# Four graph layers on one core: where VectorE pools gathered neighbours, and where one pair's keys are made

## What is computed

```python
# layer 0: maximum over the first 25 neighbours of each node
scores = where(adj != 0, -arange(N), -inf)
vals, idx = top_k(scores, 25)
agg = max over the 25 of x[idx]          # missing ones are -inf
agg = where(degree <= 25, maximum(agg, 0), agg)
out = relu(concat([x, agg]) @ W + b)
# layers 1 and 2: graph attention (softmax of masked leaky_relu scores, elu)
# layer 3: attention weights from x @ att_W @ x.T, masked by adj == 1, softmax;
for W, b in ((W0, b0), (W1, b1)):        # two attention steps with the same weights
    x = tanh(att @ (x @ W + b))
```

## Time and profile before

| what | value |
|---|---|
| median of 3 runs | 1952.48 us (1941.37 to 1954.05) |
| the profiled execution's own time | 1933.09 us |
| its span, first to last instruction | 1931.0 us |
| mean granted TensorE clock | 0.952 of full speed |
| PE / PEld busy | 1671.2 us (87%) / 1316.0 us (68%) |
| DVE busy | 1429.5 us (74%) |
| ACT busy | 1127.9 us (58%) |
| POOL busy | 1445.9 us (75%) |

### The profile page before, as it was taken

The page is one execution under the profiler, slowest core; times in us unless marked ns, Lnnn a source line. Parts: engine busy times, 40 slices in busy tenths (PEclk is TensorE's granted clock), DMA queues, the critical chain, the costliest instruction groups (busy, mean ns, idle before and its releaser), DMA issues.

```text
span 1931.0 us, 29391 instructions
## 1 busy us (share of the span) xinstructions
PE 1671.2 (87%) x9767; PEld 1316.0 (68%) x9812; DVE 1429.5 (74%) x3427; ACT 1127.9 (58%) x1517; POOL 1445.9 (75%) x2135
## 2 busy tenths in 40 slices
PE   4777798999889898999989899998989898896777
PEld 2655676777759676677758677686757777595747
DVE  5874888768877789768886788768887688746531
ACT  6664755656665765656565665558556665652252
POOL 6888888888888888888788888888878887870000
PEclk9998899989999999998999999998999999997889
DMA  7231424343343333344233333435233522311010
GB/s 195 71 84 37 103 78 100 90 125 78 77 131 73 103 78 98 107 99 111 73 119 86 102 79 76 129 77 127 72 102 87 121 57 63 107 36 33 1 66 12
DMA packets 153282, 167.06 MB, mean 87 GB/s; under 512 B 102685, under 2 KB 119978, under 8 KB 153130
## 3 DMA queue, kind: packets, MB, share of 16 engines
q1 hardware_dynamic: 119594, 96.43, 18.6%
q0 software_dynamic: 33536, 68.75, 13.5%
HBM read 140.45 MB, written 4.19 MB: 75 GB/s over the span
## 4 chain that ended last, share of the span: by engine, by line
PE 43%; DVE 27%; ACT 9%; POOL 8%; issue 7%; DVEq 6%; DMA 1%; ACTq 0%; SPq 0%; POOLq 0%
PE spare L903 11%; PE big L1150 6%; POOL gathered L563 6%; PE big L1011 5%; DVEq L73 4%; PE big L1087 3%; PE big L935 3%; DVE probs_t L1454 3%; PE big L1109 3%; DVE pooled L1327 3%; ACT hot L632 2%; PE side L1127 2%; POOL pause L568 2%; DVE keys L1224 2%; PE big L1002 2%
## 5 line engine op out<-in xcount | busy, mean ns | idle before, releaser
L563 POOL DMA_INDIRECT gathered<-in_x_dram,rows x1048 | 1089.3, 1039 | 240.1 <-issue 158.4
L903 PE MATMUL spare<-hot,x_part 128*128 128x512 f32 x1552 | 393.4, 405 | 36.2 <-DVE hot L1375 27.3
L568 POOL MEMSET pause<- 32x256 bf16 x1048 | 349.9, 334 | 41.9
L903 PEld LDWEIGHTS spare<-hot,x_part 128*128 128x128 f32 x1552 | 291.4, 193 | 108.9 <-issue 21.2
L632 ACT ACTIVATE hot<-running,minus_count 128x2048 fp32r<-128x2048 bf16 (+1 forms) x131 | 251.1, 1916 | 131.8 <-PE spare L903 112.8
L635 ACT ACTIVATE hot<-hot,plus_one 128x2048 fp32r<-128x2048 f32 (+1 forms) x131 | 251.5, 1920 | 4.3
L1011 PEld LDWEIGHTS big<-values,probs_t 128*128 128x128 f32 x1792 | 219.8, 199 | 8.6
L1011 PE MATMUL big<-values,probs_t 128*128 128x129 f32 x1792 | 222.7, 283 | 0.4
L1327 DVE TENSOR_REDUCE pooled<-gathered 128x128 f32<-128x2048 f32 (+2 forms) x56 | 212.0, 3786 | 14.3 <-DMA gathered<-in_x_dram,rows 13.3
L1375 DVE TENSOR_SCALAR hot<-running 128x2048 fp32r<-128x2048 bf16 (+1 forms) x145 | 186.4, 1305 | 33.9 <-PE spare L903 16.4
L1454 DVE SCALAR_TENSOR_TENSOR probs_t<-side,col_gain,adj_t 128x1024 f32<-128x1024 f32 x128 | 154.6, 1276 | 27.3 <-ACT side L691 27.3
(11 more groups left out here) (203 smaller groups left out, 2629.5 us busy)
## 6 DMA issues: line engine op xcount, KB each, us to landing
adj_in<-in_adj_dram SPq DMA_DIRECT2D x128, 512.0 KB, 3.7
gathered<-in_x_dram,rows POOLq DMA_INDIRECT x1048
xs<-in_x_dram SPq DMA_DIRECT2D x8, 512.0 KB, 4.7
out_dram<-xs SPq DMA_DIRECT2D x8, 512.0 KB
adj_t<-adj_bf SPq DMA_TRANSPOSE x64
packed_t<-group_bits SPq DMA_TRANSPOSE x28, 2.8
w_sb<-in_L_gnn_W_dram SPq DMA_DIRECT2D x1, 128.0 KB
w_sb<-in_L_gnn_W_dram SPq DMA_DIRECT2D x2, 64.0 KB
```

Source lines behind the costliest of these rows:

```text
L563: (late_gathered if late else rows_gathered[t % RING]).raised_by(pool.indirect_dma_start(out=gathered[:, t % RING, k * C:(k + 1) * C], out ...
L568: last = nc.gpsimd.memset(pause[quarter:quarter + 32, k // (4 * PAUSED), :], 0.0)
L903: last = nc.tensor.matmul(pick_bank(b, q), x_parts[part][:, m, :], hot[:, place_of(b, q, m), :], start=(m == 0 and part == 0), stop=(m == ...
```

## The change

Three of the poolings move, and one pair's packing and keys.

- Pool 4 moves from "steps" into the attention loop, a new place "tile 5" behind the row maximum of tile 5.
- Pool 6 moves from "last step" to the end of "steps", ahead of `max_pick` 11.
- Pool 7 moves from "end" to "last step", and that place moves: it now stands behind hot 13 and ahead of `max_pick` 13.
- The keys of pair 1 move. They were made for graph b+1 in graph b's "layer 0"; now they are made for graph b+2 in graph b's second attention step, at a new place "turned" behind `max_pick` 13. For graph 1 they are made in the start (`FIRST_WORK` 22).
- PE's packing for them moves from behind tile 7 of the second step to behind tile 1, ahead of pick 13; ACT's `take_fed` 3 moves to directly behind the conversion, ahead of hot 14.
- With "end" empty, the layer norm stands ahead of `max_pick` 15.

```diff
--- before.py
+++ after.py
@@ -101,12 +101,12 @@
               17: [("members b", 1, 0), ("members c", 1, 0)],
               18: [("pool", 0, 4)],
               20: [("pool", 0, 5)],
+              22: [("keys", 1, 1)],
               24: [("pool", 0, 6)],
               26: [("pool", 0, 7)]}
 FEED_PLACE = {0: 0, 1: 1, 2: 2, 3: 7}
 FEED = {0: (1, 2), 1: (1, 3), 2: (2, 0), 3: (2, 1)}
-SIDE = {"layer 0": [("keys", 1, 1)],
-        "gat 1": [("members", 1, 1)],
+SIDE = {"gat 1": [("members", 1, 1)],
         "gat 1 heads": [("keys", 1, 2), ("pool", 1, 0)],
         "gat 2": [("members", 1, 2)],
         "gat 2 heads": [("pool", 1, 1), ("keys", 1, 3)],
@@ -115,9 +115,10 @@
         "tile 1": [("members b", 1, 3)],
         "tile 2": [("members c", 1, 3), ("pool a", 1, 3)],
         "tile 3": [("pool b", 1, 3)],
-        "steps": [("pool", 1, 4), ("keys", 2, 0), ("members", 2, 0), ("pool", 1, 5)],
-        "last step": [("pool", 1, 6)],
-        "end": [("pool", 1, 7)]}
+        "tile 5": [("pool", 1, 4)],
+        "steps": [("keys", 2, 0), ("members", 2, 0), ("pool", 1, 5), ("pool", 1, 6)],
+        "last step": [("pool", 1, 7)],
+        "turned": [("keys", 2, 1)]}
 
 
 def gathered_slots(b, t):
@@ -764,6 +765,7 @@
                     first_ready.raised_by(nc.scalar.copy(xt[:, halves[h]], side[:, halves[h]]))
                 take_xw(b, 1, high_t)
                 feed(b, slot, 3, in_loop)
+                take_fed(b, 3, in_loop)
                 if exists(b, 1, B, in_loop):
                     make_hot(b + 1, 14)
                 act.wait_ge(first_ready.sem, first_ready.at(b, 2))
@@ -774,7 +776,6 @@
                     last = nc.scalar.activation(head[:, t, :], low_t[:, t, :], ACT.Tanh, scale=recip[:, t:t + 1])
                     if t % HALF == HALF - 1:
                         att_tanh.raised_by(last)
-                take_fed(b, 3, in_loop)
                 if exists(b, 2, B, in_loop):
                     for j in range(T):
                         take_count(b + 2, 0, j)
@@ -1151,11 +1152,12 @@
                                                 start=(m == 0), stop=(m == T - 1))
                     if t % HALF == HALF - 1:
                         att_heads.raised_by(last)
+                    if t == 1 and exists(b, 2, B, in_loop):
+                        feed(b, slot, 3, in_loop)
                     if t in (1, 5) and exists(b, 1, B, in_loop):
                         spare_maxed(b + 1, 12 + t // HALF)
                         pick(b + 1, 13 + t // HALF)
                 if exists(b, 1, B, in_loop):
-                    feed(b, slot, 3, in_loop)
                     pick(b + 1, 15)
                     if exists(b, 2, B, in_loop):
                         spare_maxed(b + 1, 14)
@@ -1502,7 +1504,6 @@
 
             def graph(b, slot, in_loop):
                 flat = xs[slot][:, :, :].rearrange("p t c -> p (t c)")
-                side_work(b, slot, "layer 0", in_loop)
                 for h in range(2):
                     dve.wait_ge(pooled_turned.sem, pooled_turned.at(b, h + 1))
                     pooled_t_ready.raised_by(nc.vector.tensor_tensor(pooled_t[:, halves[h]], high[:, halves[h]],
@@ -1543,11 +1544,13 @@
                 if picks:
                     max_pick(b + 1, 11)
                     make_hot(b + 1, 12)
-                side_work(b, slot, "last step", in_loop)
                 if picks:
                     max_pick(b + 1, 12)
                     make_hot(b + 1, 13)
+                side_work(b, slot, "last step", in_loop)
+                if picks:
                     max_pick(b + 1, 13)
+                side_work(b, slot, "turned", in_loop)
                 for h in range(2):
                     dve.wait_ge(att_tanh.sem, att_tanh.at(b, 2 + h + 1))
                     link(nc.vector.tensor_tensor(
@@ -1558,10 +1561,9 @@
                         if picks:
                             make_hot(b + 1, 15)
                             max_pick(b + 1, 14)
-                side_work(b, slot, "end", in_loop)
+                layer_norm(slot)
                 if picks:
                     max_pick(b + 1, 15)
-                layer_norm(slot)
 
             def pack_first():
```

## The result

The changed kernel takes 1980.35 us (median of four runs, 1975.45 to 1985.73) where the kernel before takes 1951.01: a ratio of 1.0163, interval 1.0128 to 1.0199, or +29.3 us. It is slower, as forecast; the forecast was 1993.5, +41.

A forecast was written before the change was run, and what follows sets the result against it. Bound mainly by the string pick 15, counts, layer norm half, `take_xt`, conversion, hot 0. Graph 0's 13.8 plus 27.5 for graphs 1 to 5 gave +41: 1952.5 + 41 = 1993.5 us, chance 0.55, range 1950 to 2014 (forecast's own 1980 to 2005).

The forecast's parts named there:

- mechanism: Second attention step: DVE stands at pool 7 for tile 7's rows, delaying `max_pick` 13, picks 14 and 15: +41 us in all.
- Its size: DVE's stand at pool 7 for gathered rows: some 12 us in each of graphs 1 to 5, 20 in graph 0.
- The landing itself: Graph 2, POOL's gathers: tile 7's last ends at 841.74, its rows land 1.6 us later, at 843.3.
- The graph's term of 5.5: Each of graphs 1 to 5 loses 4.6 to 6.2 us, taken as 5.5: 27.5 together.
- The lucky profile: Whole span: the profiled execution's 19.4 us below the median was taken as common to both kernels, giving 1993.5 instead of 1974.
- Graph 0: Second step: POOL's rate alone sets it; pick 14 comes 14.6 us later, less 0.8: +13.8.
- Graph 6: No packing or keys behind; wait alike, but pool 7 no longer ahead of its layer norm: 0, bounds -4 and +6.
- The packing: Ahead of pick 13: PE stands 0.9 us for the transpose, bounds 0 and 5.0, hidden by pool 7's wait: cost 0.
- Layer norm and L1508: Graph's end and layer 0: ACT's 0.36 us wait goes; L1508 no longer holds PE 2.06 us, but none comes through.
- Rival C: Waits ahead of picks 14 and 15 halve PE's clock, each pick 5.43 instead of 3.89 us: +18, 2012; chance 0.17.
- B's condition: Pool 7: rows landed by 838, so `max_pick` 13 is done when PE reaches pick 14; not slower, 1942; chance 0.16.
- D: Tile 7's gathers at 1.55 us, landing at 840: a graph +2, graph 0 +10, 1972 us; chance 0.12.

The follow-up runs named there:

- e11: The changed kernel with the pair's packing moved from ahead of pick 13 to behind it: 1979.60 us, 1.0104 of the kernel before.
- e14: The change with packing, `take_fed` and keys at their old places, POOL's pause behind each gather 336 elements instead of 256: 2029.93 us, 1.0340 of the kernel before.
- e2: The kernel before with pool 7 alone moved, ahead of `max_pick` 13: 2033.31 us, 0.9992 of the kernel before.
- e4: The changed kernel with packing, `take_fed` and keys at their old places, usual pause: 2013.05 us, 0.9946 of the kernel before.
- e8: The kernel before, unchanged, run again for a second profile: 2032.22 us, ratio 0.9992.
- e9: The kernel before with the pair packed behind tile 1 and taken early by ACT, keys left at layer 0: 2043.22 us, 1.0113 of the kernel before.
- the first two groups: Follow-up runs on two chips, where the kernel before took 2036 us and 2024 us.
- e12: The kernel before with POOL's pause behind each gather 336 elements instead of 256: 1976.53 us, 1.0093 of the kernel before.

## Why the prediction was right, and where its steps were off

- **Direction: right; mechanism: right in part.** Pool 7 stands for tile 7's rows in every graph, as forecast, and `max_pick` 13, the keys, the residual sum and hot 15 queue behind it; POOL's wait at tile 4 grows. e11 shows that the change costs without the packing's stand, and its pick 14 waits behind pool 7; e14's cost is pool 7's and pool 6's together. But in the profile after pool 7's stand is the later one in graphs 0, 1 and 5 alone.
- **Its size was too large.** I took 12 us in graphs 1 to 5 and 20 in graph 0; they were 9.7, 7.0, 9.8, 7.0 and 11.2, and 12.6. The landing itself was computed well: from POOL's first gather of tile 4 to tile 7's pooling there are 867.10 - 762.52 = 104.6 us after, 843.3 - 739.11 = 104.2 in the forecast. What I held fixed and should not have is the second step's start. It came 2.9, 8.4, 0.0, 7.9 and 2.0 us later behind L1058 in graphs 1 to 5, 4.2 in the mean, with ACT's wait above, and POOL's first gather of tile 4 only 0.4 in the mean. So the stand was 8.9 us in the mean and not 12. The graph's term of 5.5 was 19.8 / 5 = 4.0, and both stands are in it.
- **The lucky profile.** I took the 19.4 us between the profile of before and its median as common to both kernels. In a kernel that waits at a place for something that doesn't slip, small slips elsewhere are absorbed; the profile of before, which lay under every other execution of its kernel, overstates the stand. This is argued from the point above; no run splits it off.
- **Graph 0: 13.8 against 13.4, by another way.** I gave pool 6 in "steps" 0 to 2 us. In graph 0 it stood 6.93 us (DVE at 380.45 after), pick 12 waited 4.6 us behind it, and pool 7 stood less than forecast.
- **Graph 6: 0 against -4.4**, just outside my bound of -4: with no keys and packing behind, the layer norm free of pool 7 gains what the forecast had left open. In e2 and e4 this stretch is 36.7 and 35.9 us too; in e8, with pool 7 at its old place, 40.6.
- **The packing: 0 as hidden, wrong.** PE's stand was not 0.9 but 2.3 to 2.8 us in graphs 1 to 5, 12.8 in all, within the bounds of 0 and 5: in graph 2 the packing ran 6.3 us behind the issue of the pair's second transpose, not 4.1. And the cover was thinner than thought: in graphs 2, 3 and 4 the packing's stand, in 2 and 3 with a slow pick 13, is the later of the two. An estimate from the rows of graphs 1 to 5: by the packing alone PE would come to pick 14 some 4.4 us later than before, by pool 7 alone (landing and 4.9 us) some 3.1. So that the sum came near is in part luck: one stand was smaller than taken, the other larger, and they cover each other. Curing the packing's (e11) leaves 1.0104; after's 1.0163, of another measurement, is 0.6% more, about 12 us. "Without that cover it costs 1 to 6 us" a graph was right: 2.9 in e9.
- **Layer norm and L1508: right, with one sign against it.** ACT's half after has no wait for DVE's offset in graph 2, and the start gains nothing. I had named L1508 on the chain as a sign of being wrong, and in graph 2 it is there (L1509 at 899.29). But pick 0's second chunk starts at 907.07, right behind hot 0's end at 907.02, as forecast.
- **Rival C (clock):** the mean granted clock is 0.955 after and 0.952 before, so over the span no lost clock shows. In places it does: pick 13 takes 5.50 us behind the packing's wait in graph 2, pick 14 6.06 in graph 0, where it waited. In e11 pick 14 takes 6.5 to 6.7 us in graphs 1, 3 and 5, behind waits of 4.4 to 4.6; in graph 1 the granted clock is 0.50 from 642 to 646 us, the 1.2 GHz level. So C is no rival there but part of pool 7's price.
- **Rivals B and D.** B's condition holds on the chips of the first two groups. D (rows half as late, 1972 us) means a stand of 840 - 831.4 = 8.6 us, and the mean was 8.9. Not by faster gathers, as D has it: the 64 still take 103 us, 1.61 each. The step came later.
- **A reading that was off:** tile 7's last gather is issued at 840.79, 1.1 us before PE is at pick 14 (841.89), not after. Nothing hangs on it.

## What to carry to other kernels

An instruction that waits for a transfer may be moved ahead on its in-order engine only as far as the landing allows: write down, from the same zero, when the data land, when the first consumer behind it is needed, and how long the work between takes; need less work (14.4 - 5.0 = 9.4 us here) is the latest landing that costs nothing. Two stands that cover each other can't be priced by removing one, so remove each alone, and make the disputed one larger: the poolings that measured -0.5% on one chip cost 2.4% on another, with POOL's gathers made some 10 us longer per graph. And where a chip's own pace moves the two sides against each other, a move to "idle" time can cost in one place and next to nothing in another: the same changed kernel measured 1.0163 where the kernel before takes 1951 us, and 1.0026 where it takes 2024 (a2).

## What had not been expected of the hardware

The kernel before took 1951, 2036, 2024 and 1960 us: in the first measurement and in the three groups, each of which agrees within 1.5% in itself. The clock explains little: 0.941 in e8 against 0.952. What differs is PE in its dense stretches of 128x128 matmuls. The groups of L1011 and L1087 (busy, mean ns of one, idle ahead of them), first in the profile before, then in e8:

```profile
L1011 PE MATMUL big<-values,probs_t 128*128 128x129 f32 x1792 | 222.7, 283 | 0.4
...
L1087 PE MATMUL big<-values,probs_t 128*128 128x128 f32 x1024 | 118.3, 274 | 0.0
```

```profile
L1011 PE MATMUL big<-values,probs_t 128*128 128x129 f32 x1792 | 245.8, 292 | 21.6 <-issue 19.9
...
L1087 PE MATMUL big<-values,probs_t 128*128 128x128 f32 x1024 | 137.3, 289 | 12.7 <-issue 11.9
```

That is 42 us more busy time and 34 us more idle time, put down to nothing that the profile shows, out of a difference in span of 92.5; beside them ACT waits 61.0 us at L752 for something "remote", 8.8 us at most. Before's list has no such wait at L752, though one of 75.3 us at L613. POOL's gathers keep their pace meanwhile (102.8 us against 102.6 for tiles 4 to 7 of graph 2), and that is what makes the rows early. The signs come in degrees: e8 has 69 places in these two groups with over 0.5 us from the start of one matmul to the next, e11 12, after 6, before and e12 to e14 none. The Trainium skill (Runtime: NRT & Kernel Launch, Instruction fetch mechanics) says that an engine's instructions are refilled in 16 KiB blocks while it runs, a cost that is mostly hidden. Both pages count the same 77 packets and 1.26 MB of such refills, and no run here shows whether the gaps have to do with them. The cause stays open.
